# Third dense stage without a stored x1, with TensorE doing its sums; the second edge layer scales rows back

## The reference

```
aggr = segment_sum(gelu((x[src] + edge_attr) @ W_pre + b_pre) * bases, dst)
y = x + aggr
h = relu(bn(y @ W1 + b1)); h = relu(bn(h @ W2 + b2))
x1 = layernorm(x + y + h)
msgs = relu(relu(x1[src] @ W_r.T + b_r) @ W_r.T + b_r)
gates = segment_sum(msgs, dst) @ W_ih.T + b_ih + b_hh
c = sigmoid(i) * tanh(g); hn = sigmoid(o) * tanh(c)
out = layernorm(x1 + (relu(relu(hn @ W1.T + b1) @ W2.T + b2) @ W3.T + b3))
```

## Time and profile before

| | us |
|---|---|
| median of 3 runs | 2319.26 |
| lowest and highest | 2314.6, 2322.12 |
| the profiled execution | 2319.4 |
| its span, first to last instruction | 2317.6 |
| PE busy | 1687.7 |
| DVE busy | 1674.6 |
| ACT busy | 1374.9 |
| POOL busy | 1331.2 |

### The profile page before, as it was taken

One profiled execution on the slowest core, in us unless ns is written; L12 is line 12 of the kernel. 1 busy time (PEld: TensorE's weight loads), 2 busy tenths in 40 slices (PEclk: granted clock), 3 DMA queues, 4 the chain that ended last, 5 costly groups with the idle time before them and its releaser, 6 DMA issues. The chain is left out here.

```text
span 2317.6 us, 29544 instructions
## 1 busy us (share of the span) xinstructions
PE 1687.7 (73%) x7615; PEld 1318.4 (57%) x7615; DVE 1674.6 (72%) x3360; ACT 1374.9 (59%) x1983; POOL 1331.2 (57%) x1204
## 2 busy tenths in 40 slices
PE   3646569999979888973333333333999999999994
PEld 2434458888856556652322222223777777777773
DVE  2646546666669888988999999993666666666662
ACT  1323325556757667756888888882565555555552
POOL 5535057750018882006999999996466666655642
PEclk8878779999989999985555555556999999999996
DMA  9999679998869999969999999985111111111110
GB/s 342 367 350 350 224 200 343 341 347 290 288 229 325 339 338 363 322 218 369 401 399 399 403 398 399 400 346 195 36 53 55 58 60 60 58 56 53 49 39 21
DMA packets 171831, 572.69 MB, mean 247 GB/s; under 512 B 27441, under 2 KB 50583, under 8 KB 170322
## 3 DMA queue, kind: packets, MB, share of 16 engines
q1 hardware_dynamic: 123282, 445.99, 50.6%
q0 software_dynamic: 47136, 73.04, 13.4%
q10 hardware_dynamic: 1344, 52.84, 6.0%
HBM read 332.27 MB, written 295.04 MB: 271 GB/s over the span
## 5 line engine op out<-in xcount | busy, mean ns | idle before, releaser
L967 PE MATMUL d_pN<-k_ident,d_r 128*128 128x128 f32 x784 | 192.6, 427 | 336.4 <-ACT d_r L982 335.7
L967 PEld LDWEIGHTS d_pN<-k_ident,d_r 128*128 128x128 f32 x784 | 153.8, 224 | 375.1 <-issue 343.9
L499 DVE BATCH_NORM_STATS2 k_stats<-d_pH 128x512 f32 (+1 forms) x392 | 253.1, 687 | 102.4 <-PE d_pH L52 100.8
L990 ACT ACTIVATE d_o<-d_u,d_nb,d_rs 128x256 f32<-128x256 f32 x392 | 203.6, 590 | 81.2 <-POOL d_nb L1026 81.2
L1033 POOL TENSOR_TENSOR d_u<-d_x,k_base 128x1024 f32<-128x1024 f32 x98 | 230.8, 2355 | 14.7 <-DVE d_x L1058 9.5
L589 POOL DMA_INDIRECT scratch_y<-k_sums,k_target x98 | 151.2, 1543 | 122.9 <-POOLq L61 68.7
L50 PE MATMUL d_pH<-d_r_h,k_w_h 128*128 128x512 f32 x392 | 164.4, 419 | 56.4 <-DVE d_r_l L828 28.0
L779 ACT ACTIVATE d_r<-d_h,d_coef 128x512 f32<-128x512 f32 x196 | 149.2, 809 | 84.6 <-DVE d_r_l L828 39.8
L636 ACT ACTIVATE d_y_h<-d_pT 128x1024 fp32r<-128x1024 f32 x98 | 100.5, 1025 | 158.7 <-PE d_pT L605 158.7
L810 POOL DMA_INDIRECT scratch_y<-k_sums,k_target x98 | 169.4, 1729 | 33.7 <-issue 19.4
L529 POOL TENSOR_TENSOR bn_rstd<-bn_var,k_minus_half 128x2 f32<-128x2 f32 x2 | 1.5, 728 | 322.5 <-DVE bn_var L516 322.5
(11 more groups left out here) (199 smaller groups left out, 5077.1 us busy)
## 6 DMA issues: line engine op xcount, KB each, us to landing
d_y<-scratch_y SPq DMA_DIRECT2D x196, 512.0 KB, 7.1
scratch_h<-d_h SPq DMA_DIRECT2D x196, 512.0 KB, 7.8
d_h<-scratch_h SPq DMA_DIRECT2D x196, 512.0 KB, 6.8
scratch_y<-in_x ACTq DMA_DIRECT2D x25, 2000.0 KB, 12.2
scratch_x<-d_x SPq DMA_DIRECT2D x97, 512.0 KB, 8.0
out<-d_o SPq DMA_DIRECT2D x97, 512.0 KB, 7.7
attr<-in_attr_t SPq DMA_DIRECT2D x25, 512.0 KB, 26.3
bases<-in_bases_t SPq DMA_DIRECT2D x25, 512.0 KB, 23.4
```

Of the source, the lines that this page charges most:

```text
L499: return dve.bn_stats(out, psum)
L967: last = pe.transpose(pN[b][:, j, cc * P:(cc + 1) * P], r[:, b, cc, j * P:(j + 1) * P], K.ident[:])
L990: last = act.activation(o[:, q, j], u[:, q, j], ACT.Identity, bias=nb[:, q, J + j:J + j + 1], scale=rs[:, q, J + j:J + j + 1])
```

## The change

1. `dense3` no longer makes or stores x1. Normalizing s = 2y + h and adding the base row gives x1 + base; the change takes s from PSUM, scales it by its root and adds the base row: u = s * rs + base. Its mean is left out, since the mean of a row of u then differs by a constant that the second norm removes (the base row's own mean and the biases of the edge layer are shifted accordingly, in `edges0`). The output row has 260 columns instead of 256 (FP): column 256 holds v * rs, the root of the variance, so that out * root gives back a row of u up to its mean.
2. TensorE makes s: two ordinary fp32 products with twice the identity (`twice`) for 2y, and eight with the identity for the turned relu, summed in PSUM. pN has four buffers instead of two.
3. Statistics are taken over pairs of rows with one `bn_stats` each: the operand runs through row 0 and row 1 alternately, element by element, and its two halves come out as the two rows' statistics; `bn_aggr` is not needed.
4. `dense3`'s loops are written out, and in a new order: VectorE does first(k+3), then second(k+1); ScalarE does normed(k), then relu(k+4); SP loads batch k+4, then stores batch k.
5. `edges0` does the base row and the bias rows inside batches SIDE = 6 to 10, in small fp32 products of 4 columns; their weights load early, into the part of `K.sums` that is still free.
6. `edges1` gathers from out. Since stores to out must not come before the gathers of source rows, POOL picks all source rows first (`pick_src`, three batches a step) into `bounce`, SP moves them out to x_src and loads them again (`load_src`); the results are held in six buffers and stored from step 6 on, three batches a step. VectorE multiplies each source row by its root before TensorE turns it (four `tensor_scalar`), and the add of the destination rows becomes four `scalar_tensor_tensor`. Marks (`has`) load batch by batch.

```diff
@@ edges0, tensor @@
+            def base_mlp(n):
+
+                pe.wait_ge(kept, SIDE + n)
+                pe.wait_ge(side_ready, n + 1)
+                if n == 0:
+                    pe.wait_ge(wm_full, 64)
+                    for ic in range(C):
+                        last = pe.matmul(pS[:, 0, 0:4], raw_m[:, ic], hid4[:, ic], start=ic == 0, stop=ic == C - 1)
...
+                if SIDE <= k < SIDE + 5:
+                    base_mlp(k - SIDE)
-
-            pe.wait_ge(gelu_done, EB)
...
@@ edges0, vector @@
+                if SIDE <= k < SIDE + 5:
+                    dve.wait_ge(side_product, k - SIDE + 1)
+                    (first_mlp, second_mlp, third_mlp, shifted_biases, bias_rows)[k - SIDE]()
@@ dense3, sync @@
+            def load(k):
+                if k >= 4:
+                    sp.wait_ge(relu_done, k - 3)
+                sp.dma_start(h2[:, k % 4], A["h2"][k]).then_inc(h2_full[k % 4], 16)
+                if k >= 4:
+                    sp.wait_ge(summed, k - 3)
+                sp.dma_start(y[:, k % 4], rows(k)).then_inc(y_full[k % 4], 16)
...
+            for k in range(NB):
+                if k + 4 < NB:
+                    load(k + 4)
+                sp.wait_ge(o_done, k + 1)
+                sp.wait_ge(root_kept, k + 1)
...
@@ dense3, tensor @@
+            for k in range(NB):
+                pe.wait_ge(y_full[k % 4], 16 * (k // 4 + 1))
+                if k >= 4:
+                    pe.wait_ge(u_done, k - 3)
+                for two in range(J // 2):
+                    pe.matmul(pN[k % 4][:, 2 * two:2 * two + 2].rearrange("p j f -> p (j f)"), twice[:],
+                              y[:, k % 4, two * 2 * F:(two + 1) * 2 * F], start=True, stop=False)
                 pe.wait_ge(relu_done, k + 1)
                 for j in range(J):
                     for cc in range(C):
+                        last = pe.matmul(pN[k % 4][:, j, cc * P:(cc + 1) * P], r[:, k % 2, cc, j * P:(j + 1) * P], K.ident[:],
+                                         start=False, stop=j % 2 == 1 and cc == C - 1)
+                last.then_inc(summed, 1)
@@ dense3, scalar @@
+            def normed(k):
+                n = (k - 1) % 4
+                act.wait_ge(nb_done, k + 1)
+                act.wait_ge(u_done, k + 1)
...
+            for k in range(4):
+                relu(k)
+            for k in range(NB):
+                normed(k)
+                if k + 4 < NB:
+                    relu(k + 4)
@@ dense3, gpsimd @@
+            for n in range(-3, NB - 1):
+                a, b, at = n + 3, n + 1, n % 4
+                now = slice(0 if real(a) else J, 2 * J if real(b) else J)
+                if real(a):
+                    pool.wait_ge(st1_done, a + 1)
+                if real(b):
+                    pool.wait_ge(st2_done, b + 1)
...
+                pool.tensor_tensor(out=rs[:, at, now], in0=v[:, at, now], in1=K.minus_half[:, now], op=ALU.pow).then_inc(rs_done, 1)
...
@@ dense3, vector @@
+            def pairs(out, rows):
+
+                for p in range(J // 2):
+                    last = dve.bn_stats(out[:, 2 * p:2 * p + 2].rearrange("p j s -> p (j s)"),
+                                        rows[:, 2 * p:2 * p + 2].rearrange("p j f -> p f j"))
+                return last
+
+            def first(k):
+                dve.wait_ge(summed, k + 1)
+                if k >= 4:
+                    dve.wait_ge(rs_done, batches(k - 7))
+                pairs(st[:, (k - 3) % 4, 0:J], pN[k % 4]).then_inc(st1_done, 1)
+
+            def second(k):
+                dve.wait_ge(rs_done, batches(k - 3))
+                if k >= 3:
+                    dve.wait_ge(o_done, k - 2)
+                for j in range(J):
+                    last = dve.scalar_tensor_tensor(out=u[:, k % 3, j], in0=pN[k % 4][:, j], scalar=rs[:, (k - 3) % 4, j:j + 1],
+                                                    in1=K.base[:], op0=ALU.mult, op1=ALU.add)
+                last.then_inc(u_done, 1)
+                dve.wait_ge(u_done, k + 1)
+                pairs(st[:, (k - 1) % 4, J:2 * J], u[:, k % 3]).then_inc(st2_done, 1)
...
+            for k in range(-3, NB - 1):
+                if real(k + 3):
+                    first(k + 3)
+                if real(k + 1):
+                    second(k + 1)
@@ edges1 @@
+        def picks(k):
+
+            first = {-2: 2, -1: 4}.get(k, 8 + 3 * k)
+            return list(range(first, min({-2: 4, -1: 8}.get(k, first + 3), EB)))
...
+            def load_src(k):
+                sp.wait_ge(moved_out[k % 2], 16 * (k // 2))
+                sp.wait_ge(turned, k - 1)
+                sp.dma_start(xs[:, k % 2, 0:tiles(k)], source_rows(k)).then_inc(xs_full[k % 2], 16)
...
+            for k in range(-2, EB):
+                if k >= 0 and k + 2 < EB:
+                    load_src(k + 2)
...
+                for n in picks(k):
+                    move_out(n)
...
+                now = picks(k)
+                for n in now[0:1]:
+                    pick_src(n)
                 if real(k - 1):
                     deviations(k - 1)
                 if real(k + 1):
                     fetch_dst(k + 1)
+                for n in now[1:]:
+                    pick_src(n)
```

560 lines of the change are left out of this document (257 added, 303 removed).

## The result

| | before | changed |
|---|---|---|
| median, us | 2319.51 (4 runs) | 2532.87 (4 runs) |
| lowest and highest, us | 2314.6, 2322.12 | 2529.23, 2542.08 |
| the profiled execution, its span, us | 2319.4, 2317.6 | 2542.08, 2540.3 |

The changed kernel takes 1.0929 times as long, 95% interval 1.0893 to 1.0964: 9% slower, where 5% was forecast. In one later case, experiment 10, one of six executions ran at a granted clock of 0.731 instead of 0.94 and took 2471.34 us; the median of 2233.97 given there counts it, the median of the other five is 2232.04, and the ratio leaves it out.

A forecast was written before the change was run, and what follows sets the result against it. Each stage had its own limit; the third dense stage, full on VectorE and DMA, would become bound by a four-engine loop. 2319.4 - 11 + 114 + 14 = 2436 us, 5.0% slower; own range 2395 to 2485, 8 in 10 range 2395 to 2540.

The forecast's parts named there:

- The bound, and the sign: Third dense stage: the new order closes a loop over POOL, ScalarE, TensorE and VectorE; whole kernel 5.0% slower, slower chance 0.87.
- First edge stage, -11: Side work moved inside batches 6 to 10 ends the stage 13.6 us earlier, less 2.4 for weights; bounds 0 and 14.
- Third dense stage, +114: Batch distance grows from 5.175 to 6.4 us, +119, less some 5 at the tail; bounds +94 and +201.
- I take 6.4: Third dense stage: us per batch chosen between 6.2 at TensorE's high clock and 7.0 at the low one.
- The sums for either clock, 12.4 and 14.0 us for two batches: Third dense stage loop of POOL, normed, relu, turned sums, VectorE's step and handoffs, at TensorE's high and low clock.
- If a load were late by 1 us, a third of that would show: Third dense stage: effect per batch of a late load, as SP issues each load behind the store before it.
- Second edge stage, +14: Multiplies ahead of the first turn +1.5, late turn(2) +10.5, later slips 2; bounds +2 and +35.
- later steps may slip 2 more: Second edge stage: steps after the late start lose 2 us, POOL's 22.8 to 27.5 us being balanced with 26.8.
- turn(2) was forecast 12 us late: Second edge stage start: batch 2's load waits behind six picks and move-outs, +10.5, and four multiplies add 1.5.
- Strided statistics at half rate: Rival, third dense stage: statistics over row pairs take double, loop 7.4 us a batch, 2533 us in all; chance 0.15.
- The clock stays low: Rival, third dense stage: granted clock stays 0.50, TensorE alone needs 7.3 us a batch, 2523 us in all; chance 0.10.
- The loop that doesn't close: Rival, third dense stage: the series hides beside one VectorE step, 4.0 us a batch, 2203 us in all; chance 0.11.

The follow-up runs named there:

- experiment 10: The kernel of experiment 7 run again unchanged, beside another variant: 2233.97 us, ratio 0.9615 to the kernel before.
- experiment 1: Changed kernel with SP's stores in the third dense stage one batch later, behind the loads of batch k+4: 2536.74 us, ratio 1.0945 to before.
- experiment 4: Changed kernel with SP's third dense stage stores two batches later and ScalarE's relu(k+4) ahead of normed(k): 2275.48 us, ratio 0.9823 to before.
- experiment 5: Changed kernel with stores one batch later and TensorE's y products of even batches done three times over: 2459.43 us, ratio 1.0617 to before.
- experiment 6: Changed kernel with POOL issuing all three picks of a second edge layer step ahead of the deviations: 2517.37 us, ratio 1.0863 to before.
- experiment 2: Changed kernel with only ScalarE's order in the third dense stage swapped, relu(k+4) ahead of normed(k): 2707.12 us, ratio 1.1694 to before.
- experiment 7: Changed kernel with the edits of experiment 4 and experiment 6, plus SP's second edge layer source loads issued earlier: 2234.2 us, ratio 0.9677 to before.
- experiment 3: Changed kernel with SP's stores one batch later and ScalarE's relu(k+4) ahead of normed(k): 2371.27 us, ratio 1.0234 to before.

## Why the prediction was right and wrong

**The bound, and the sign: right.** The change was forecast slower because an order closes a loop over four engines, and the trace shows the loop link by link (experiment 1). Opening it together with the loop through SP turns 9% slower into 1.8% faster (experiment 4).

**First edge stage, -11: too small.** It was -15.8, beyond the bound of -14. The side work left the tail as forecast, 13.6 us. The term of 2.4 us for the weights that load among other traffic did not show: the last scan starts at 280.58 us, 1.9 earlier than in the earlier trace rows, not later. Why it is earlier was not tested.

**Third dense stage, +114: the step that failed is "I take 6.4".** The links were sized well: TensorE's turned sums 2.05 and 3.65 against 2.05 and 3.68 measured, normed and relu to the hundredth. Two errors cancelled, which is luck: POOL took 2.4 and not 2.62, and four scaled adds took 1.64 and not 1.4, so VectorE's step is 4.24 and not 3.98. The sums for either clock, 12.4 and 14.0 us for two batches, are what experiments 5 and 1 measured. Wrong was the choice between them. The prediction weighed TensorE's busy share and the mean granted clock of the stage; but what counts is the clock in those sums that lie in the loop, and in experiment 1 these are the ones behind the long wait, each time. The wait was put at 2.5 us and is 3.9 to 5.1 there. So a mean clock of 0.82 goes with a batch at the low clock's price, 6.9 to 7.0. The step taken as 6.4 misses 97 x (6.97 - 6.4) = 55 us, which is all that the forecast of this stage lacked; its ends gave back 5.6 us, as forecast. For experiment 1 the cause is shown. For the changed kernel itself it is in part argued: there y can be late too, the slow products are more often those of y (37 of 91 groups at 3.0 us or more) than the turned sums (10 of 91), and by its sum below the loop through SP would be left at some 6.4 us even with a high clock. No experiment keeps the clock high with the stores as they are.

**"If a load were late by 1 us, a third of that would show": the loop behind it was not seen.** The forecast noted that SP issues each load behind the store before it, and did not follow this round. TensorE waited 193.6 us for y, and taking the wait away gave nothing (experiment 1), since the other loop was 7 us long as well. The sum for this second loop, from rows of the changed kernel: store, two loads and landing 6.35 us, TensorE 4.0 to 5.7, VectorE 4.24, POOL 2.4, normed 2.0, so 19 to 21 us for three batches, 6.3 to 6.9 each before handoffs.

**Second edge stage, +14: the step that failed is "later steps may slip 2 more".** POOL's work per step was summed and found to fit, 22.8 to 27.5 us in 26.8. But POOL's order has two picks behind the deviations, and these wait for VectorE; with SP's load behind the move-outs that is a loop again. It cost 30.6 us over five steps (164.6 against 5 x 26.8), and in experiment 6 these five steps took 27.2 us each. The start: turn(2) was forecast 12 us late. It was 38.8 late here; in experiment 2, which has the same second edge stage and a gap of only 32.5 us at its start, it came 60 us behind the stage's start, 16 late. The other 22 or so go with the late signals, which no row of before could show. The steady step is 27.2 and not 26.8, 0.4 us in each of the others; before, four of the later steps took 28.4 and now one takes 28.7, which gives back 5.

**The rivals.** Strided statistics at half rate: cleared, 693 and 688 ns against 688 along a row. (Its argument from the earlier trace rows was none: the rate of 0.60 us was itself taken from the difference of the two rows that it was then said to fit.) The Trainium skill, page "Advanced Engine Details and Errata", section Memory Cachelines, expects a penalty for reads that change lines each time; no row here shows one for this form. The clock stays low: not as put, for the granted clock was 0.82 and not 0.50, and TensorE had 240 us to spare. But its price, 7.3 us per batch and 2523 us in all, is near what came, because the burst that lies in the loop did run low. The loop that doesn't close was wrong as said, and was right as a promise: with two orders changed the batch takes 4.28 us against 4.0 there (experiment 4). The measured 2532.9 lies near the upper end of the range for 8 in 10, and in part by luck: the forecast's own range ended at 2485, and the rest up to 2540 was there for two rivals, of which one did not happen and the other only in part. Two of the three stage terms fell outside their own bounds (-15.8 against 0 to -14, +71.1 against +2 to +35).

## What to carry to other kernels

Where an engine waits inside a loop, price the burst behind the wait at the clock that it finds there, not at the mean of the stage. When a wait is removed and nothing changes, look for a second loop of the same length before calling the wait harmless: here the edits alone gave 0 and +174 us, both together -162. An edit that opens one loop can also close a shorter one, as experiment 2 did. For each in-order queue, list what stands behind a waiting instruction: a store ahead of the next load and an output ahead of the next relu cost 257 us together (2532.9 against 2275.5), more than the 114 us that the lighter work was to save.

## What the runs showed of the hardware

- In experiment 1 TensorE's low clock after waits of 3.9 to 5.1 us cost 1.6 us in each second batch; 3.3 us of useless products in that wait (5.32 against 1.98) made the kernel 77 us faster, with the granted clock of the stretch at 1.00 instead of 0.82.
- BATCH_NORM_STATS2 over 512 elements that alternate between rows 1 KB apart took 693 ns in SBUF and 688 in PSUM, as long as along a row in PSUM (688).
- At the start of the second edge stage, ScalarE and SP went on up to 28 us after the products of TensorE that they waited for were recorded as done, in some executions and not in others of the same program. VectorE did so too: in experiment 6 it took up at 1787.03 sums recorded as done by 1769.8. In experiment 7 the profiled time with such waits was 31 us above the median (2265.6 against 2234.2), so a stage's start is better compared over several profiles. They do not explain the 9.2 us by which the changed kernel's profiled execution is above its median: in experiments 1, 3 and 4 the profiled execution had them and lay within 2 us of the median. The same third dense stage took 11 us less in experiment 6's profile (6.86 us a batch against 6.97), so that spread lies there at least in part.
